# Two graph layers in one pass over the adjacency matrix: whole-row unpack, one merged bias product, catch-up in halves of 64 columns, and reordered ends

## The reference

```python
def _L0_gnn_ref(X, adj, W, b):
    deg = jnp.clip(jnp.sum(adj, axis=1, keepdims=True) + 1.0, 1.0, None)
    h_neigh = (adj @ X + X) / deg
    z = jnp.concatenate([X, h_neigh], axis=1) @ W + b
    out = jax.nn.relu(z)
    norm = jnp.linalg.norm(out, axis=1, keepdims=True)
    return out / jnp.maximum(norm, L2_EPS)

def _L1_gnn_ref(features, adj, W):
    deg = jnp.sum(adj, axis=1, keepdims=True)
    neigh = adj @ features / (deg + 1.0)
    return jnp.concatenate([features, neigh], axis=-1) @ W.T

x = _layernorm(x + _L0_gnn_ref(x, adj, L0_gnn_W, L0_gnn_b), axis=-1)
x = _layernorm(x + _L1_gnn_ref(x, adj, L1_gnn_W), axis=-1)
```

## Time and profile before

| | |
|---|---|
| median of 3 runs | 792.74 us (792.49 to 793.36) |
| the profiled execution | 794.09 us |
| its span, first to last instruction | 792.3 us |
| PE busy | 697.7 us (88%) |
| DVE busy | 709.1 us (90%) |
| ACT busy | 621.0 us (78%) |
| POOL busy | 201.7 us (25%) |
| DMA | 274.56 MB, mean 347 GB/s |

### The profile page before, as it was taken

One profiled execution on the slowest core, in us unless ns is written; L12 is line 12 of the kernel. 1 busy time (PEld: TensorE's weight loads), 2 busy tenths in 40 slices (PEclk: granted clock), 3 DMA queues, 4 the chain that ended last, 5 costly groups with the idle time before them and its releaser, 6 DMA issues.

```text
span 792.3 us, 28217 instructions
## 1 busy us (share of the span) xinstructions
PE 697.7 (88%) x11285; PEld 638.3 (81%) x11285; DVE 709.1 (90%) x2687; ACT 621.0 (78%) x848; POOL 201.7 (25%) x302
## 2 busy tenths in 40 slices
PE   1477868888898889999999999999999999999992
PEld 0467757777787778888889989899999989889992
DVE  4699977989999999999999999989999989878894
ACT  4798887989898989898988889787878889740037
POOL 2262513535413133334222030201102020201024
PEclk9988896989999999999999999999999999999997
DMA  9999999999999999999999999999999999800004
GB/s 304 388 419 419 419 419 401 408 420 410 421 417 416 415 416 395 421 393 421 390 417 385 404 381 393 372 344 384 345 411 361 404 350 368 314 2 2 2 15 96
DMA packets 46121, 274.56 MB, mean 347 GB/s; under 512 B 12642, under 2 KB 12706, under 8 KB 13218
## 3 DMA queue, kind: packets, MB, share of 16 engines
q1 hardware_dynamic: 45184, 270.55, 86.3%
q0 software_dynamic: 576, 2.10, 0.7%
q10 hardware_dynamic: 226, 0.07, 0.0%
HBM read 270.60 MB, written 2.10 MB: 344 GB/s over the span
## 4 chain that ended last, share of the span: by engine, by line
PE 48%; DVE 29%; issue 8%; DMA 6%; POOL 5%; ACT 3%; ACTq 0%; DVEq 0%; POOLq 0%; SPq 0%
PE s_ps L360 22%; DVE e L737 10%; PE u_ps L378 7%; DVE t_sb L744 6%; PE p_ps L346 6%; DMA a_in<-in_adj 3%; POOL small L1088 3%; PE z_ps L396 3%; DMA xl<-in_x 3%; PE z_ps L393 3%; PE z_ps L417 2%; DVE u_sb L744 2%; PE u_ps L428 1%; PE p_ps L428 1%; DVE a_in L744 1%
## 5 line engine op out<-in xcount | busy, mean ns | idle before, releaser
L542 ACT ACTIVATE junk<-a_in 128x2048 uint8<-128x2048 uint16 x256 | 489.2, 1918 | 4.0 <-DMA a_in<-in_adj 4.0
L360 PE MATMUL s_ps<-xh,t_sb 128*128 128x129 f16 x4096 | 386.7, 250 | 18.6 <-DVE t_sb L744 15.5
L360 PEld LDWEIGHTS s_ps<-xh,t_sb 128*128 128x128 fp8e4 x4096 | 311.3, 102 | 48.4 <-DVE t_sb L744 19.4
L737 DVE TENSOR_SCALAR e<-a_in 128x2048 fp8e4<-128x2048 f32 x256 | 310.2, 1222 | 8.2 <-DMA a_in<-in_adj 7.7
L1096 POOL COPY store<-pk 128x32 uint32<-128x32 uint32 (+1 forms) x250 | 119.8, 521 | 313.2 <-ACT pk L551 313.2
L346 PE MATMUL p_ps<-pow_bf,e 128*128 128x16 bf16 x4096 | 142.5, 170 | 51.7 <-DVE e L737 48.8
L346 PEld LDWEIGHTS p_ps<-pow_bf,e 128*128 128x128 fp8e4 x4096 | 128.6, 97 | 68.8 <-DVE e L737 62.7
L744 DVE TENSOR_SCALAR t_sb<-pk 128x128 uint32<-128x128 uint32 x1024 | 150.8, 219 | 6.5 <-ACT pk L551 6.0
L1088 POOL TENSOR_TENSOR small<-small,minus_half 128x4 f32<-128x4 f32 x32 | 65.3, 2040 | 228.0 <-DVE small L798 176.4
L378 PE MATMUL u_ps<-xh,u_sb 128*128 128x128 f16 x1488 | 99.1, 218 | 0.0
L378 PEld LDWEIGHTS u_ps<-xh,u_sb 128*128 128x128 fp8e4 x1488 | 88.9, 97 | 1.2
(11 more groups left out here) (102 smaller groups left out, 512.6 us busy)
## 6 DMA issues: line engine op xcount, KB each, us to landing
a_in<-in_adj SPq DMA_DIRECT2D x256, 1024.0 KB, 8.9
xl<-in_x POOLq DMA_DIRECT2D x4, 512.0 KB, 15.8
out_h<-e SPq DMA_DIRECT2D x8, 256.0 KB, 2.6
w_sb<-in_L_gnn_W ACTq DMA_DIRECT2D x1, 32.0 KB
w_raw<-in_L_gnn_W ACTq DMA_DIRECT2D x1, 32.0 KB
b_sb<-in_L_gnn_b ACTq DMA_DIRECT2D x1, 0.2 KB
```

Of the source, the lines that this page charges most:

```text
L360: last = nc.tensor.matmul(s_ps[:, n % 2, at:GW], t_sb[:, b, :], xh[:, b, at:GW], start=(b == 0), stop=False)
L542: nc.scalar.activation(junk[:, t % 2, :], halves[t % R], ACT.Copy, scale=1.0 / 128, accum_out=half_sum[:, n, c:c + 1]).then_inc(s_half, 1)
L737: nc.vector.tensor_scalar(e8[:, c, :], a_in[:, t % R, :], 1.0, None, ALU.is_equal, saturate=False).then_inc(s_e, 1)
```

## The change

Five things change. The unpack of a row becomes one call of 8 instructions over the whole row, with two buffers `t_sb`; it stands behind `compare(n, 1)`, and TensorE's sums move by a quarter: quarter 3 of row n-2 behind the first pack of row n, quarters 0 to 2 of row n-1 behind the others. `catch_up` moves to chunks 2 and 3, `unpack_piece` behind `compare(n, 2)`. The bias is split into three bf16 rows that sum to it, and enters the dense layer by one matmul of 256 columns ahead of the four products, in place of one fp32 matmul for each. `catch_up` multiplies every block by its 64 high and then its 64 low columns into the same 64 PSUM columns, so that `add_piece` has one addition. At the start the transposes of the second layer's weights stand behind the first row's packs; at the end the last variance and half of the last scaling are VectorE's, and variances are taken one step later.

```diff
@@ sum_quarter @@
-                if i % 2 == 0:
-                    pe.wait_ge(s_t, n * 2 + i // 2 + 1)
+                if i == 0:
+                    pe.wait_ge(s_t, n + 1)
...
-                    last = nc.tensor.matmul(s_ps[:, n % 2, at:GW], t_sb[:, b, :], xh[:, b, at:GW],
+                    last = nc.tensor.matmul(s_ps[:, n % 2, at:GW], t_sb[:, n % 2, b, :], xh[:, b, at:GW],
@@ catch_up @@
-                        last = nc.tensor.matmul(u_rows[:, r, :], u_sb[:, r * W + b, :],
-                                                xh[:, low(q - 1) + b, 0:HP], start=(b == 0), stop=(b == W - 1))
+                        for part in range(2):
+                            last = nc.tensor.matmul(u_rows[:, r, 0:F], u_sb[:, r * W + b, :],
+                                                    xh[:, low(q - 1) + b, part * F:(part + 1) * F],
+                                                    start=(b + part == 0), stop=(b + part == W))
@@ dense @@
-                dense_products(cat_t, w0_sb, True).then_inc(s_zps, 1)
+                if e == 0:
+                    pe.wait_ge(s_b0, 1)
+                nc.tensor.matmul(z_flat[:, 0:BR * F], ones_bf[:, :], b0_rows[:, :, :].rearrange("p k f -> p (k f)"),
+                                 start=True, stop=False)
+                for k in range(BR):
+                    last = nc.tensor.matmul(z_flat[:, k * F:(k + 1) * F], cat_t[:, k, :], w0_sb[:, :],
+                                            start=False, stop=(k == BR - 1))
+                last.then_inc(s_zps, 1)
@@ tensor, the loop @@
+            for c in range(NC):
+                pack_chunk(0, c)
+            pe.wait_ge(s_w, 80)
...
-            for n in range(NB):
+            for n in range(1, NB):
...
-                    if n:
-                        sum_quarter(n - 1, c)
+                    if n > 1 or c:
+                        sum_quarter(*quarter(n, c))
...
-                    if n >= START[1] and c in (1, 2):
-                        catch_up(n, c - 1)
+                    if n >= START[1] and c >= 2:
+                        catch_up(n, c - 2)
@@ scalar @@
+            for i in range(3):
+                act.dma_start(b0_sb[i:i + 1, :], b0.unsqueeze(0)).then_inc(s_w, 16)
...
                 sum_codes(n, 0)
+                if n:
+                    take_packed(n - 1, 1)
                 if e >= 0 and k == 2:
                     take_z(e)
...
-                if n:
-                    take_packed(n - 1, 1)
...
-                for k in range(TG):
+                for k in range(TG if g < NV - 1 else TG // 2):
@@ vector @@
+            def bias():
+
+                link(nc.vector.memset(ones_bf[:, :], 1.0))
+                link(nc.vector.tensor_copy(b0_rest, b0_sb[:, :]))
+                link(nc.vector.memset(b0_sum, 0.0))
+                for i in range(3):
+                    link(nc.vector.tensor_copy(b0_part, b0_rest))
+                    link(nc.vector.tensor_copy(b0_one, b0_part))
+                    link(nc.vector.scalar_tensor_tensor(out=b0_sum, in0=b0_one, scalar=ident[0:3, i:i + 1],
+                                                        in1=b0_sum, op0=ALU.mult, op1=ALU.add))
+                    link(nc.vector.tensor_tensor(b0_rest, b0_rest, b0_one, ALU.subtract))
+                nc.vector.tensor_copy(b0_rows[:, :, :], b0_sum.unsqueeze(1).to_broadcast([3, BR, F])
+                                      ).then_inc(s_b0, 1)
...
+            def unpack(n):
+
+                dve.wait_ge(s_pk, n * 2 + 2)
+                if n >= 2:
+                    dve.wait_ge(s_sum, n - 1)
+                dst = words(t_sb[:, n % 2, :, :])
...
-                link(nc.vector.tensor_tensor(rows, u_rows[:, 0:r1 - r0, 0:F], rows, ALU.add))
-                nc.vector.tensor_tensor(rows, u_rows[:, 0:r1 - r0, F:HP], rows, ALU.add).then_inc(s_uadd, 1)
+                nc.vector.tensor_tensor(rows, u_rows[:, 0:r1 - r0, 0:F], rows, ALU.add).then_inc(s_uadd, 1)
@@ vector, the loop @@
                 compare(n, 0)
-                if n:
-                    unpack(n - 1, 0)
                 if e >= 0 and k == 3:
                     normalise(e)
-                if n > START[1]:
-                    add_piece(n - 1)
                 compare(n, 1)
...
-                if n >= START[1]:
-                    unpack_piece(n)
+                if n:
+                    unpack(n - 1)
+                if n > START[1]:
+                    add_piece(n - 1)
                 if e >= 0 and k == 2:
                     norm(e)
                 compare(n, 2)
+                if n >= START[1]:
+                    unpack_piece(n)
...
-                if n:
-                    unpack(n - 1, 1)
@@ vector, the end @@
             for g in range(NV):
+                if g >= 2:
+                    variance(g - 2)
+                if g == NV - 1:
+                    variance(g - 1)
                 add_tail(NV + g)
                 if g + 12 < 2 * NV:
                     unpack_tail(g + 12)
-                if g:
-                    variance(g - 1)
-            variance(NV - 1)
+            last_variance()
+            last_finish()
```

More of the change, by code:

```diff
@@ L157, in gnn_kernel @@
         w0_sb = sb("w0_sb", [P, F], F32)
-        w1_raw = sb("w1_raw", [F, P], F32)
         w1_sb = sb("w1_sb", [P, F], F32)
         w2_sb = sb("w2_sb", [F, 2 * F], F32)
-        b0_sb = sb("b0_sb", [1, F], F32)
+        b0_sb = sb("b0_sb", [3, F], F32)
+        b0_rows = sb("b0_rows", [3, BR, F], BF16)
+        ones_bf = sb("ones_bf", [3, P], BF16)
+        h_t = cat_t[0:F, :, :]
+        b0_rest, b0_sum, b0_one = (q_sb[0:3, i, :] for i in range(3))
+        b0_part = q_sb[0:3, 3, 0:F // 2].bitcast(BF16)
         x_in = xl[:, :, 0:F]
@@ L375, in catch_up @@
                 half = (r1 - r0 + 1) // 2
[L376 removed]
+                for r in (range(half), range(half, r1 - r0))[half_of]:
                     for b in range(W):
[L378 to L379 removed]
+                        for part in range(2):
+                            last = nc.tensor.matmul(u_rows[:, r, 0:F], u_sb[:, r * W + b, :],
+                                                    xh[:, low(q - 1) + b, part * F:(part + 1) * F],
+                                                    start=(b + part == 0), stop=(b + part == W))
                     if r == r1 - r0 - 1:
@@ L675, in _ @@
             take_g(e)
-            for g in range(NV + 1):
-                if g < NV:
+            for g in range(NV):
+                if g < NV - 1:
                     squares(g)
@@ L879, in variance, with last_variance, last_finish @@
                                                in1=fvar[:, 0, rows], op0=ALU.mult, op1=ALU.add).then_inc(s_fvar, 1)
+            def last_variance():
+                dve.wait_ge(s_vadd, 2 * NV)
+                dve.wait_ge(s_fvar, NV - 1)
+                for n in range(NB - TG, NB):
+                    ins = nc.vector.scalar_tensor_tensor(out=sqf[:, (NV - 1) % 4, n % TG, :], in0=acc[:, n, :], scalar=1.0,
+                                                         in1=acc[:, n, :], op0=ALU.mult, op1=ALU.mult,
+                                                         accum_out=fvar[:, 1, n:n + 1])
+                link(ins)
+                rows = slice(NB - TG, NB)
+                nc.vector.scalar_tensor_tensor(out=fvar[:, 1, rows], in0=fvar[:, 1, rows], scalar=1.0 / F,
+                                               in1=fvar[:, 0, rows], op0=ALU.mult, op1=ALU.add).then_inc(s_fvar, 1)
+            def last_finish():
+                dve.wait_ge(s_froot, NV)
+                dve.wait_ge(s_out[(NV - 1) % 4], 16)
+                for n in range(NB - TG // 2, NB):
+                    ins = nc.vector.tensor_scalar(o_sb[:, (NV - 1) % 4, n % TG, :], acc[:, n, :], fvar[:, 1, n:n + 1], None,
+                                                  ALU.mult)
+                ins.then_inc(s_o_dve, 1)
             def verdict():
@@ L931, in _ @@
                     weights()
+                if n == 2:
+                    bias()
                 if 2 <= n < 6:
@@ L940, in _ @@
             e = NE - 1
-            unpack(NB - 1, 0)
+            unpack(NB - 1)
             add_piece(NB - 1)
-            unpack(NB - 1, 1)
             dve.wait_ge(s_half, NB * NC)
```

61 lines of the change are left out of this document (31 added, 30 removed).

## The result

The changed kernel takes 798.68 us (median of 7 runs, 795.56 to 801.3), the kernel before on the same chips 792.6 us: ratio 1.0072, 95% interval 1.0046 to 1.0098. It is 0.7% slower; 778 was forecast. The profiled execution took 801.3 us, with a span of 799.5 us against 792.3.

What follows compares the result with a forecast made beforehand. Input DMA bounds the first group, VectorE with DMA slightly behind the next four, TensorE's instruction stream the later ones. Stream -11.6, the group from 680.02 -1.4 and tail -1.9 sum to -14.9 us off 792.74: about 778, range 768 to 790.

Steps and rivals of the forecast that it cites:

- What becomes late: At each group's fourth block, TensorE waits 1.5 us for the whole-row unpack, 2.2 where 32 blocks are wide.
- T+1.0: Start of norm on VectorE 1.0 us after the dense layer's end, where it was 0.52 us before.
- Bias: Dense layer: one bf16 matmul replaces eight fp32 passes, saving 1.34 us of TensorE per group.
- The clock: Behind dense layers TensorE's clock stays at 2.4 GHz, worth 1.7 us each time it fell before.
- the clock still falls: Rival: falls continue beside TensorE's new wait; 786 us if five in TensorE-bound groups, 790 at all seven; chance 0.18.
- Catch-up: Catch-up on TensorE: 64-column matmuls nearest 28 ns, so 1 ns more a pair, 0.15 us per group.
- slower rival: Catch-up in blocks 36 to 63: gain used up if a 64-column matmul costs over 35 ns; chance 0.09.
- VectorE: VectorE relieved by 0.9 to 1 us per block; four groups of 41.2 us fall to 40.1, -4.4 us.
- Ends and last groups: Start 0; last four groups 181.6 to 178.9 us; the group from 680.02 -1.4 us; tail -1.9 us.

Runs made afterwards that it cites:

- 780.6 us kernel: Changed kernel with, in each fourth block, normalise behind the whole-row unpack, and transpose_h, dense_h, take_h and take_g later: 780.62 us, ratio 0.9866.
- 776.0 us kernel: Kernel before with the merged bias and the 64-column catch-up with one add, in the old order: 776.02 us, ratio 0.9815.
- 780.8 us kernel: 776.0 us kernel with two row buffers, sums one chunk later and h in shared buffers, row still unpacked by halves: 780.79 us, ratio 0.9858.

## Why the prediction was wrong

The step that failed is *What becomes late*: "the whole-row unpack at the fourth block of a group", priced as a wait of TensorE of 1.5 to 2.2 us, with VectorE's slack of over 1 us in the next block, for which it shows no row, taken to end the matter. Where it is alone the wait itself was rather smaller than booked (1.06 us). The path was followed from the dense layer to the first wide sum and left there. Behind that sum stand `dense_h` and, in ScalarE's order, `take_g`, all later chunks' codes and the next packed half, which the next row's unpack needs. I took ScalarE's chain only for T+1.0 and never asked whether it has slack; in the turn above it has 1.2 us in 24. What the runs showed in its place is a loop: waits for the packed half of 25.7 us, for g of 22.2 and for the row of 16.4 in the seven middle groups (2.5, 6.6 and 5.5 before), which last 305.3 us where 286.1 were forecast; the row unpacked whole, in its new place, costs over 90 us by itself (872.3 against 780.8), and h and g a step later give 18 us of the changed kernel back.

*Bias* was right in kind and booked too small. The dense layer takes 1.15 us (643.70 to 644.85), not 1.56, since the eight fp32 passes now take 0.119 us each; from 200 us on no slow stretch stands directly behind a dense layer any more. Alone it gave 11.6 us. Between the profiled spans (792.3 and 777.3) 4.6 us lie before the copy of the third z, where the forecast had put nothing.

*The clock.* The forecast took all falls of the later seven groups as gone. In the last four they are: 1.00 after 0.98. In the three before they moved from the dense layer to TensorE's waits: 0.95 after 0.96, which at half speed is 0.05 x 136.1 = 6.8 us where 0 was booked. In the four before them it is 0.95 after 0.98, 8.5 us against 3.3. So the rival that "the clock still falls" came true in the middle, and at the place it named. All falls of the three groups begin behind TensorE's wait for the whole row, which follows the fp32 transposes and a short pack; two of them, waits first, then windows:

```profile
431.25 3.55 PE L373 MATMUL s_ps<-xh,t_sb 128*128 128x257 f16 x16 [1.06 <-DVE t_sb L786]
...
475.90 3.50 PE L373 MATMUL s_ps<-xh,t_sb 128*128 128x257 f16 x16 [1.06 <-DVE t_sb L786]
...
431.50:434.90 3.40, 3.40 (x17) 2.15 (x16) 3.40 (x11) 0.61 (x3) 0.00 (x0) 0.52 0.99 393
475.90:479.30 3.40, 3.40 (x16) 2.23 (x16) 3.40 (x11) 0.86 (x3) 0.00 (x0) 0.52 1.10 376
```

The same wait of 1.06 us at 658.41 has no fall behind it, so the wait alone doesn't decide. By these counts the clock makes up at most 12 of the 19 us by which the seven groups exceed the forecast (an estimate: 6.8, and 8.5 less 3.3). How much of it is really clock and how much waiting I can't part; with later h and g both are less (0.97 and 0.99).

*Catch-up.* 32 matmuls of 64 columns take 0.95 us (650.59 to 651.54), 29.7 ns each; the pair is 59 ns, about 3 over the forecast, and far under the 35 ns a matmul at which the slower rival would decide. The Trainium skill ("TensorE: Matmul & The Clock Gate", "Weight-path perf modes — Fast Weight Load (FWL) and DoubleRow") has 40 ns for small fp8 matmuls; the trace disagrees. The edit as a whole gave 3 us, which I put down to the add that VectorE no longer does; no run parts the two.

*VectorE.* The relief is there, 13.3 us in four groups; the step from it to groups of 40.1 us was not borne out. The 780.6 us kernel, with the same relief and h and g later, still needs 40.9 a group there, and the 776.0 us kernel, with only the add gone, 41.1.

*Ends and last groups.* The dense layer to the end gave 1.1 us for 1.9, the group before it 0.3 for 1.4, the last four groups -0.1 for 2.7. The groups from 599.2 and 643.9 have the forecast's 44.7; the two before them last 46.8 and 45.5.

By the table the miss is 22.1 us of span. Of it 19.2 lie in the two middle stretches (305.3 us where 286.1 were forecast); the start is 2.7 better and the rest 5.6 worse. Moving h and g later gives back 18 us, more than the 6 that were lost against before, because the gain of bias and catch-up then reaches the end.

## What to carry over

Where two or three engines work in a fixed order, follow a late item past the first wait, until it comes back to the engine that made it late: here it cost where the loop closed through an engine with 1.2 us of slack in 24, and nothing in the 776.0 us kernel. A bigger unit of hand-over (a row for two halves) saves instructions on one engine and makes every consumer wait for the last of its inputs, so its place matters too; here 34 us less work on VectorE (692.9 us in the 776.0 us kernel, 658.7 after) came with 20 us more time. When a change bundles edits, price each by itself: bias and catch-up alone give 776.0 us, 1.9% under the kernel before and the version to keep.

## What the runs showed of the hardware

The fp32 passes of 64 columns take 0.119 us in a run of eight alike (0.95 us, above), and 0.181 where passes of one row stood between them.

GpSimd's copies of packed bits change length from kernel to kernel: the same 250 copies take 849 ns each on average in the 776.0 us kernel, 521 before and 377 after. VectorE's busy time alone doesn't order them (692.9, 709.1 and 658.7 us). In the timeline of the 780.8 us kernel one copy spans 0.26 us, another of the same shape 5.97:

```profile
585.53 1.21 DVE L777 TENSOR_SCALAR t_sb<-pk 128x128 uint32<-128x128 uint32 x8 [0.35 <-ACT pk L570]
586.00 0.26 POOL L1130 COPY store<-pk 128x64 uint32<-128x64 uint32 x1
...
606.37 5.97 POOL L1130 COPY store<-pk 128x64 uint32<-128x64 uint32 x1 [6.90 <-ACT pk L570]
...
606.59 1.22 DVE L770 TENSOR_SCALAR e<-a_in 128x2048 fp8e4<-128x2048 f32 x1
607.73 1.17 DVE L777 TENSOR_SCALAR t_sb<-pk 128x128 uint32<-128x128 uint32 x8
608.81 2.36 DVE L770 TENSOR_SCALAR e<-a_in 128x2048 fp8e4<-128x2048 f32 x2
611.08 1.17 DVE L777 TENSOR_SCALAR t_sb<-pk 128x128 uint32<-128x128 uint32 x8
612.88 0.42 DVE L808 TENSOR_TENSOR xl<-u_ps,xl 128x256 f32<-128x256 f32 x1 [0.63 <-PE u_ps L389]
```

The long copy ends at 612.34, 0.09 us into the first gap that VectorE has (from 612.25). That fits the Trainium skill ("SBUF — State Buffer", section "SBUF: two separate sides", on the shared port pair: an exclusive lock, under which the loser blocks). The short copy doesn't fit as well, since VectorE is at an unpack beside it. Spans on GpSimd are rough, and no run here takes VectorE's work away to test it. The long copies cost nothing that shows: no wait for them stands among the waits of these kernels.
